# Score stack of a fused two-layer block: rows in another order, other loads, another plan

## The reference

```
x = layernorm(x + attention(x));  x = layernorm(x + ffn_fp4(x))
x = layernorm(x + mamba(x));      x = layernorm(x + ffn_lora(x))
```

## Time and profile before

| | us |
|---|---|
| median of 3 runs | 953.11 (951.97 to 953.21) |
| profiled execution | 947.06 |
| its span | 945.3 |
| PE busy / DVE busy | 661.9 / 638.6 |
| ACT busy / POOL busy | 428.6 / 345.2 |

### The profile page before, as it was taken

One profiled execution on the slowest core, in us unless ns is written; L12 is line 12 of the kernel. 1 busy time (PEld: TensorE's weight loads), 2 busy tenths in 40 slices (PEclk: granted clock), 3 DMA queues, 4 the chain that ended last, 5 costly groups with the idle time before them and its releaser, 6 DMA issues.

```text
span 945.3 us, 12082 instructions
## 1 busy us (share of the span) xinstructions
PE 661.9 (70%) x3939; PEld 403.1 (43%) x3939; DVE 638.6 (68%) x1230; ACT 428.6 (45%) x896; POOL 345.2 (37%) x328
## 2 busy tenths in 40 slices
PE   3248664896769775878589676977588668866455
PEld 1124343543535454435454453545444454444124
DVE  1725067587868586877858686858688667855581
ACT  1212432582548253743458154825374327622532
POOL 5512122291319222653238131922265004500550
PEclk9995977899888988897889987898789779966795
DMA  4111110231043201320123104320142003100310
GB/s 128 60 79 42 61 47 28 105 118 79 1 132 104 84 15 46 143 102 41 46 109 106 71 0 132 103 84 13 46 147 94 40 14 128 54 1 6 135 44 7
DMA packets 39871, 65.99 MB, mean 70 GB/s; under 512 B 6705, under 2 KB 29058, under 8 KB 37506
## 3 DMA queue, kind: packets, MB, share of 16 engines
q1 hardware_dynamic: 37666, 64.57, 19.8%
q10 hardware_dynamic: 2176, 1.05, 0.4%
HBM read 57.68 MB, written 7.86 MB: 69 GB/s over the span
## 4 chain that ended last, share of the span: by engine, by line
PE 43%; DVE 28%; DMA 11%; issue 10%; ACT 5%; POOL 1%; SPq 1%; DVEq 0%; ACTq 0%; POOLq 0%
PE ps_s L1036 14%; PE ps_f L1036 8%; PE ps_v L1036 8%; DMA x_tm<-in_L_attn_x_dram 6%; PE ps_n L1036 6%; PE ps_y L1036 6%; DVE mx L897 4%; DMA stack_mem<-stack_dram 3%; DVE shared L997 3%; DVE x L834 2%; DVE y_out L834 1%; DVE bn L821 1%; DVE newton L814 1%; PE ps_f L1040 1%; DMA lmem<-x 1%
## 5 line engine op out<-in xcount | busy, mean ns | idle before, releaser
L581 POOL TENSOR_TENSOR shared<-u,bcrow 128x1024 f32<-128x1024 f32 x64 | 199.2, 3117 | 145.0 <-DVE u L986 94.4
L897 DVE TENSOR_REDUCE mx<-ps_s 128x2 f32<-128x512 f32 (+1 forms) x192 | 127.4, 687 | 81.1 <-PE ps_s L1036 79.7
L997 DVE TENSOR_TENSOR_SCAN shared<-ps_f,shared 128x512 f32<-128x512 f32 x128 | 149.9, 1209 | 43.8 <-PE ps_y L1036 19.3
L1036 PE MATMUL ps_s<-stack_mem 72*128 72x128 bf16 (+3 forms) x1024 | 156.0, 275 | 10.4 <-ACT probs L669 4.9
L1036 PE MATMUL ps_y<-shared,ident 128*128 128x512 f32 x256 | 123.7, 613 | 30.6 <-DVE shared L1002 30.5
L752 ACT ACTIVATE ps_f<-delta,amat 128x255 f32<-128x255 f32 x256 | 109.6, 473 | 50.4 <-DVE shared L997 30.1
L669 ACT ACTIVATE probs<-ps_s 128x512 f32<-128x512 f32 x192 | 105.0, 594 | 35.6 <-PE ps_s L1036 34.2
L1036 PEld LDWEIGHTS ps_s<-stack_mem 74*128 74x128 bf16 (+1 forms) x1024 | 88.6, 109 | 69.3 <-issue 23.7
L1036 PEld LDWEIGHTS ps_y<-shared,ident 128*128 128x128 f32 x256 | 44.5, 192 | 84.1 <-DVE shared L1002 48.1
L1002 DVE TENSOR_TENSOR shared<-shared,bcrow 128x1024 f32<-128x1024 f32 x64 | 78.4, 1225 | 2.2
L1036 PE MATMUL ps_s<-causal,ident_bf 128*128 128x256 bf16 (+1 forms) x192 | 66.9, 357 | 7.7 <-DVE mx L897 3.9
(11 more groups left out here) (205 smaller groups left out, 1045.7 us busy)
## 6 DMA issues: line engine op xcount, KB each, us to landing
bcrow<-bc_dram SPq DMA_DIRECT2D x64, 512.0 KB, 4.0
stack_mem<-stack_dram SPq DMA_DIRECT2D x16, 576.0 KB
stack_mem<-stack_dram SPq DMA_DIRECT2D x48, 192.0 KB
stack_dram<-parts SPq DMA_DIRECT2D x24, 256.0 KB, 3.0
x_tm<-in_L_attn_x_dram ACTq DMA_DIRECT2D x8, 128.0 KB, 9.3
xb<-in_L_attn_x_dram SPq DMA_DIRECT2D x8, 128.0 KB, 2.1
out_dram<-y_out SPq DMA_DIRECT2D x8, 128.0 KB, 1.9
fmem<-in_L_attn_conv_w_dram SPq DMA_DIRECT2D x1, 512.0 KB
```

What stands on the lines that cost most here:

```text
L581: G.tensor_tensor(bx[:, j % 2], u[:].unsqueeze(2).to_broadcast(S4), bcrow[:, j % RING, 0].unsqueeze(1).to_broadcast(S4), ALU.mult).then_in ...
L897: V.tensor_reduce(mx[:, a, min(i, 1), hd[0]:hd[-1] + 1:2], ps_s[:, n % 2].rearrange("p (h n) -> p h n", h=len(hd)), AX.X, ALU.max).then_in ...
L997: V.tensor_tensor_scan(hs[:, j % HB, c].rearrange("p n t -> p (n t)"), ps_f[:, c, :], bx[:, j % 2, c].rearrange("p n t -> p (n t)"), 0.0, ...
L1036: return nc.tensor.matmul(o, lhsT, rhs, start=start, stop=stop, **kw)
```

## The change

The rows of the stack get another order: partition 3k + i instead of 24i + k, the same for both sides, so that the nine pairs of parts still meet. Each side is now loaded by three transfers of 24 rows, to every third partition. The source pattern begins with the eight numbers of a head and then runs over the three parts (key side) or repeats one part three times (query side). So there are six transfers for each a instead of four, and the semaphore counts are 96 instead of 64 a sequence.

```diff
-                    sp.dma_start(stack[0:KROWS, 2 + a].rearrange("p h n -> p (h n)"),
-                                 stack_dram[2 + a].rearrange("i (d h) n -> (i d) (h n)", d=DH).unsqueeze(0).to_broadcast([3, 3 * DH, H * T])).then_inc(stack_r[a], 16)
-                    for i in range(3):
-                        rows = slice(i * 3 * DH, (i + 1) * 3 * DH)
-                        sp.dma_start(stack[rows, a].rearrange("p h n -> p (h n)"),
-                                     stack_dram[a, i].rearrange("(d h) n -> d (h n)", d=DH).unsqueeze(0).to_broadcast([3, DH, H * T])).then_inc(stack_r[a], 16)
+                    for side in (2 + a, a):
+                        for i in range(3):
+                            src = stack_dram[side].rearrange("i (d h) n -> d i (h n)", d=DH)
+                            if side == a:
+                                src = src[:, i].unsqueeze(1).to_broadcast([DH, 3, H * T])
+                            sp.dma_start(stack[i:KROWS:3, side].rearrange("p h n -> p (h n)"), src).then_inc(stack_r[a], 16)
```

Some of the due times behind it:

```diff
     "pool": {
-        "core": [-2, 52],
+        "core": [-2, 43],
...
     "pe": {
-        "scan": [68, 71.6, 75.6, 89.5, 93, 100.7, 105.7, 109.4],
-        "norm_std": [97.4],
+        "scan": [68, 71.6, 75.6, 86.2, 89.7, 97.5, 102.5, 106.4],
+        "norm_std": [104.7],
```

More of the change, by code:

```diff
@@ L40 @@
     "sp": {
-        "lora_ffn": [27.4, 49.9],
+        "lora_ffn": [26.4, 59.4],
         "prep": [45.8, 57.7, 61.4, 63.8, 97.9, 101.2],
-        "core": [52.8, 55.9, 56.2, 75, 85.5],
+        "core": [52.8, 55.9, 56.2, 75, 80.2],
         "rows": [68.7, 71.2, 71.5, 71.8, 72.1, 82.9, 87.2, 90.1, 93.8],
@@ L46 @@
     "pool": {
-        "core": [-2, 52],
+        "core": [-2, 43],
         "prep": [15.5, 28.9, 40.6, 44.3],
-        "lora_ffn": [29.2],
+        "lora_ffn": [31.2],
         "mamba": [68.9],
@@ L54 @@
         "prep": [0, 10.4, 12.8, 14.2, 16.4, 17.9, 19.1, 25.9, 38, 42.3],
-        "core": [0.3, 68.9, 69.5, 70, 70.5, 71, 73.2, 73.7, 75, 76.2, 76.8, 77.3, 80, 83.6, 84.2, 84.7, 85.2, 87.3,
-                 87.8, 88.3, 90.9, 91.5, 92, 93.7, 94.3, 95.2, 97.1],
+        "core": [0.3, 68.9, 69.5, 70, 70.5, 71, 72.7, 73.2, 74.5, 75.8, 76.3, 78.7, 82.6, 84.4, 84.9, 85.5, 85.6,
+                 86.8, 87.4, 87.9, 90.5, 91, 91.5, 93.3, 93.8, 94.7, 96.6],
         "norm": [12.1, 14.6],
-        "mamba_out": [17.2],
+        "mamba_out": [14.8],
         "lora_ffn": [22, 32.9, 41.9],
         "ffn": [25.7, 28.8, 41.1, 45.7],
-        "mamba": [49.1, 52.1, 58.1, 62.2, 63.8],
-        "scan": [67.4, 68.2, 74.2, 75.5, 78, 79.2, 81.7, 82.9, 85.7, 86.5, 89, 90.1, 96.3, 97.6, 100.4, 101.6],
+        "mamba": [49.1, 51.3, 57.3, 62.2, 63.8],
+        "scan": [67.4, 69, 71.4, 75.5, 78, 79.2, 81.7, 82.9, 85.7, 86.5, 89, 92.1, 96.3, 97.6, 100.4, 101.6],
     },
@@ L65 @@
         "mamba_out": [3.7, 10.3, 14.8],
-        "norm": [4.6, 7.8, 11.7],
+        "norm": [4.6, 7.8, 11.5],
         "core": [5.5, 6.2, 9, 9.7, 20.4, 21, 22.5, 24.3, 25.8, 34.1, 34.7, 36.7, 40.5, 45.6, 46.2, 47.4, 53.8, 55.5,
@@ L69 @@
         "ffn": [15.8, 17.4, 17.8, 18.4, 19.4, 26.6, 29.4, 30.3, 31.4, 33.3, 39.2, 41.3],
-        "prep": [19.7, 21.6],
-        "lora_ffn": [23.1, 25.1, 35.3, 37.4],
-        "mamba": [44.5, 52.5, 60.9],
+        "prep": [20.9, 22.3],
+        "lora_ffn": [23.9, 25.9, 36.2, 36.3],
+        "mamba": [44.6, 49.9, 60.9],
         "scan": [67.3, 68.5, 69.7, 71.3, 72.5, 73.8, 75, 76.2, 77.5, 78.6, 79.8, 81.1, 82.3, 83.5, 84.7, 89.6, 90.8,
-                 92.1, 93.7, 94.9, 97.3, 98.7, 99.9, 101.2],
+                 92.1, 93.3, 94.5, 97.3, 98.7, 99.9, 101.2],
         "norm_std": [110.4],
@@ L78 @@
         "norm": [0, 2.2, 3.7],
-        "prep": [0.9, 3, 3.8, 5.7, 7.3, 7.4, 23.1],
-        "core": [1.4, 1.9, 4.1, 5.1, 7.5, 7.6, 17.7, 20.3, 21.5, 24.7, 25.2, 32, 35.5, 35.6, 37, 43, 49.7, 50.1, 51,
+        "prep": [0.9, 2.8, 3.9, 5, 6.6, 9.2, 25.8],
+        "core": [0.8, 1.9, 4.1, 5.1, 7.3, 7.6, 17.7, 20.3, 21.5, 24.7, 25.2, 32, 35.5, 35.6, 37, 43, 49.7, 50.1, 51,
                  52.8, 53.4, 54.7, 55, 55.9, 56.6, 57.8, 57.9, 58.6, 60.1, 60.7, 61.3, 62, 63.3, 64.1, 64.4, 64.9,
[L82 to L87, removed]
-        "scan": [68, 71.6, 75.6, 89.5, 93, 100.7, 105.7, 109.4],
-        "norm_std": [97.4],
+                 65.5, 66, 66.7, 69.7, 70.4, 73.8, 74.2, 74.5, 75.1, 77.3, 77.7, 78, 78.7, 80.8, 81.2, 81.5, 82.4,
+                 84.6, 84.9, 85.3, 85.6, 86.9],
+        "mamba_out": [6],
+        "lora_ffn": [13.5, 15.9, 21.6, 24, 26.1, 28],
+        "ffn": [16.6, 19.2, 22.5, 22.6, 30.4, 32.8],
+        "mamba": [42.2, 44.9, 50.7, 51.8],
+        "scan": [68, 71.6, 75.6, 86.2, 89.7, 97.5, 102.5, 106.4],
+        "norm_std": [104.7],
     },
@@ L411, in prep @@
                         for a in range(2):
-                            sp.wait_ge(stack_r[a], f * 64)
+                            sp.wait_ge(stack_r[a], f * 96)
                     sp.dma_start(stack_dram[:, i].rearrange("t p n -> p t n"), parts[:, i]).then_inc(stack_w, 16)
@@ L1112, in core @@
                     if n % 12 == 0:
-                        pe.wait_ge(stack_r[a], f * 64 + 64)
+                        pe.wait_ge(stack_r[a], f * 96 + 96)
                     if n == 0 and not is_first(f):
```

## The result

| | before | after |
|---|---|---|
| median of 4 runs, us | 953.16 (951.97 to 956.91) | 896.25 (891.78 to 897.78) |
| profiled execution, us | 947.06 | 895.68 |
| its span, us | 945.3 | 893.9 |

The ratio is 0.9389 (0.9346 to 0.9432): 6.1% faster. The predicted 915 was 18.7 us too high, and the result lies 0.75 us under the low end of the range. It is nearest to the rival "full yield" (903). The low end is missed by less than the four runs spread (6 us), so what needs an explanation is the 18.7 us. Profile against profile the gain is 51.4 us, where the sum said 38.2.

The account below looks back on a forecast made before the run. The prediction took the kernel as a relay between PE, DVE and ACT, with DMA a ninth of the chain. Loads 28.6 plus orders 9.6 made 38.2 us off the profiled 947.06, about 908.9; plus 6.05 gave 915, range 897 to 936.

Parts of the forecast that it names:

- full yield: Rival: loads as forecast, all of the orders, full clock after the boundary (about 1 more a turn); 903, chance 0.20.
- Start: Before PE's first QK: the stack pair lands near 47 and x_tm near 52, gaining about 5 us.
- (d): Turn -1: two QK groups fill PE's 1.25 us wait for POOL's linesn; 1.3 us.
- Turn 0: Boundary to turn 0: x_tm comes 4.4 us earlier and the first QK group fills PE's wait; 5.3 us.
- Ordinary boundary: Boundaries to turns 1 to 5: combine matmuls begin earlier; 3.0 us each (bounds 1.8 to 5), 15 in all.
- The charge for moutw: On PE after the boundary: moutw's matmuls stand behind prep's qk matmuls; up to 1.1 us lost.
- Turn 6: PE's 4.71 us idle for the lmem load falls to an ordinary turn's 1.39; 3.3 us.
- Loads in all: Sum of the load terms for start, turn 0, turns 1 to 5 and turn 6; 28.6 us.
- (a) y_out: POOL's xb add precedes the last parts subtraction, so DVE's y_out takes 0.6, not 2.47; 1.25 a turn, 6.3 in all.
- (b) dbc: PE does two QK groups before the dbc matmuls, so DVE's reduces start earlier; 1.0 a turn, seven turns, 7 us.
- (c) fourth scan addition: Fourth scan accumulation moves before the last weighted product, cutting DVE's 2.77 us idle; 0.65 a turn, 4.6 in all.
- bounds 0 and 19.2, I take half, 9.6: Order terms total 19.2 us; read singly on old start times, one can eat another, so 9.6 was counted.

Follow-up runs that it names:

- loads_only: The new loads with all due times of the kernel before; 922.47 us, ratio 0.9728.
- moutw_back: The changed kernel with moutw's matmuls ahead of prep's qk matmuls on PE again; 896.06 us, ratio 0.9422.
- fourth_back: The changed kernel with PE's fourth scan addition behind the last weighted product again; 901.35 us, ratio 0.9509.
- act_old: The changed kernel with ACT's old order of decay factors and exponentials in the scan stage; 903.39 us, ratio 0.9535.
- dbc_back: The changed kernel with mamba's dbc matmuls ahead of the two score groups on PE again; 914.67 us, ratio 0.9628.
- three_first: The changed kernel with stack rows ordered by part first, so source patterns begin with 3, still six transfers; 915.38 us, ratio 0.9629.

## Why the prediction was 19 us too high

- **Engines of the load: right.** Eight at 25 GB/s (27 each were forecast). x_tm lands in 6.0 us, not 3 to 5: the stack is still moving beside it (until about 491 us at the boundary to turn 4). At the ordinary boundaries that costs nothing, in after or in loads_only: PE does not wait for it.
- **Start: wrong.** 5 us were put down for the loads. loads_only gains 0.55 up to turn 0's load: both pairs are on the eight engines when x_tm is issued, it lands after 10.6 us and not near 52, and PE takes it at 55.41, later than before (53.70). What it saves is the wait for the stack behind it. With the new plan 4.2 us are gained, where start and (d) were to give 6.3.
- **Turn 0: right.** loads_only is 5.3 shorter there, as forecast. In after, 4.71 us of x_tm wait are left (2 to 4 forecast) and the turn is 7.85 shorter, where the wait, dbc and the scan step were to give 6.95.
- **Ordinary boundary: right in size,** 3.33 by 3.0. The charge for moutw inside it was wrong (moutw_back: nothing).
- **Turn 6: right,** 4.71 to 1.32 is 3.4 by 3.3.
- **Loads in all: right but for the start.** 28.6 forecast, 24.4 by loads_only; without the start 23.6 and 23.8.
- **(a) y_out: right,** 1.27 a turn by 1.25. Nothing came of POOL's longer wait for xb.
- **(b) dbc: size off.** The wait for the first reduce fell by 1.53, but delta came only 0.61 earlier, not 1.0. Putting it back costs another 6.0 us over seven turns in the scan stage, where PE's clock differs.
- **(c) fourth scan addition: the mis-sized term.** Forecast 0.65 a turn (its own times, 516.84 less 516.15, give 0.69), 4.6 in all; measured 15.8 over seven turns for the whole scan stage. Two errors stand in it. `fourth_back` makes the move itself worth 7.7 there, and not 4.6. And the prediction took the 1.5 us DVE idle that the earlier ACT step removes for hidden, worth nothing; `act_old` makes ACT's new order worth 10.1. The two overlap, both undone cost 12.6, and dbc_back's 6.0 shows that the scan gains from the dbc move too. This stage holds 11.2 of the 13.2 us that the profile-to-profile sum was short.
- **The step that failed: "bounds 0 and 19.2, I take half, 9.6".** No mechanism stood behind the half. The terms lie in different stretches of the turn, one after another on the path, and the runs showed 27.0 us for the plan on the new loads (16.9 without them). Taken whole, the sum was 47.8, by a measured 51.4; that it comes so near is in part luck, since the loads' terms were 4.2 too high and the orders' 7.8 too low.
- **The rival "full yield"** was the nearer one, and its sum is off as well: 47.8 and "about 1 more a turn" for five turns are 53, and 50 were taken off; the 1 us of clock is also in the 3.0 of the boundary already. So 903 is no better founded than 915.
- **Lost, and not forecast:** the convolution's 16 matmuls took 6.22 us after and 5.19 before in turn 4, their start at half clock, which makes that stretch 0.5 us longer on average of five turns, and the stretch to hff cost 1.8 us over five turns. The forecast had PE gain clock at the boundary (it did: the combine matmuls take 1.0 us, not 1.7) and lose none elsewhere.
- **The offset.** 6.05 us were added because the timed median lay that much above the profiled execution. After's median lies 0.57 above its own. Before's medians in the later calls were 948.3 to 952.2 and its single runs 943.5 to 959.2, so its profile had caught one of the shorter executions. That is 5.5 of the 18.7 us; the other 13.2 are the orders.

## What to carry to other kernels

Read the leading count of a DMA's source pattern: here 3 meant three engines, and the small load that followed paid for the backlog. Try loads and order of consumers apart and together: here they gave 41.3 us apart and 51.4 together, and most of the difference that could be placed was PE's clock in one stretch. Don't halve a sum of terms that lie one after another on the path: discount a term only for a named reason, and check whether "hidden" idle time is still hidden once its neighbour has gone.

## What the runs showed of the hardware

- PE's granted level in one stretch of short matmuls and short waits went between 1.00 and 0.50 from turn to turn of the same loop, with 7.0 to 10.0 us for the stretch. Edits elsewhere that move work by 2 us or less a turn changed how many turns were slow. So the price of an undone edit here holds up to 7.6 us (10.6 for the pair) that aren't its own, or hides 3.4 to 3.6, and four of them (8.6, 7.1, 5.1, 18.4) add up to 39 us, more than the 26.2 that lie between loads_only and after.
- Filling 2.3 us of PE's idle time with unread matmuls moved the fall of the clock in dbc_back and didn't remove it; the time stayed the same there (912.95 against 914.67) and in the changed kernel (896.03 against 896.25).
- A contiguous 3 by 8 pattern ran at a share of 0.66 and 205 GB/s (three_first), the 8 by 3 one at 0.50 and 200 GB/s, the 3 by 8 broadcast at 0.19 and 75 GB/s, all 192 KB each.
